# First-layer weights of all eight experts loaded during the routing and kept in SBUF; second-layer weights in two buffers; new order of the splits and additions

## The reference

```python
router_probs = jax.nn.softmax(flat @ router_w + router_b, axis=-1)
topk_probs, topk_idx = jax.lax.top_k(router_probs, 2)
...
# for each of the two experts e of a token, weighted by its probability:
gelu(flat @ rw1[e] + rb1[e]) @ rw2[e] + rb2[e]     # 1024 -> 256 -> 1024
```

## Time and profile before

| | us |
|---|---|
| median of 3 runs | 3153.91 (3153.67 to 3155.99) |
| the profiled execution | 3143.41 |
| its span, first to last instruction | 3141.5 |
| routing in it | 2641 to 2695 |
| expert stage in it | 2696 to 3141.5 |

### The profile page before, as it was taken

How to read it: one execution, slowest core, us unless ns; L and a number is a source line. 1 busy time by engine, 2 the same in 40 slices (tenths; PEclk the granted TensorE clock), 3 DMA queues, 4 the chain that set the end, 5 groups by cost and what they waited for, 6 DMA issues and landing times. The chain is left out here.

```text
span 3141.5 us, 50069 instructions
## 1 busy us (share of the span) xinstructions
PE 2774.9 (88%) x13690; PEld 2153.1 (69%) x13690; DVE 2489.0 (79%) x5349; ACT 1571.3 (50%) x3053; POOL 1639.9 (52%) x1473
## 2 busy tenths in 40 slices
PE   4999969999996997998988999999999595599997
PEld 3788734444445776776766788888888484488886
DVE  8656769999997676577777999999999785577775
ACT  3555623333334525333333677777777451266664
POOL 1788746666663572777773444444444230044443
PEclk9999989999998998999999999999999797699999
DMA  5433489999992032111111778778877551499997
GB/s 184 113 93 107 143 303 347 348 350 353 349 335 59 1 134 55 36 23 23 22 23 34 260 261 259 260 260 261 260 263 255 175 201 58 183 297 297 289 293 194
DMA packets 193609, 609.60 MB, mean 194 GB/s; under 512 B 41979, under 2 KB 51570, under 8 KB 189758
## 3 DMA queue, kind: packets, MB, share of 16 engines
q0 software_dynamic: 135040, 429.23, 43.3%
q1 hardware_dynamic: 58430, 178.63, 16.2%
HBM read 522.69 MB, written 84.86 MB: 193 GB/s over the span
## 5 line engine op out<-in xcount | busy, mean ns | idle before, releaser
L649 POOL DMA_INDIRECT g_rows<-z_rows,edge_src x704 | 696.6, 990 | 608.5 <-PE g_totals L1473 314.7
L1090 POOL DMA_INDIRECT shared<-el_rows,edge_src x352 | 336.7, 957 | 179.6 <-issue 107.0
L690 ACT ACTIVATE g_scaled_hi<-g_rows,edge_weight_sorted 128x1024 fp32r<-128x1024 f32 x176 | 202.7, 1151 | 355.3 <-DMA g_rows<-z_rows,edge_src 345.3
L704 PE MATMUL g_sums<-g_rows,g_share 128*128 128x512 f32 x704 | 332.2, 594 | 22.9 <-DMA g_rows<-z_rows,edge_src 22.9
L1466 PE MATMUL g_sums<-g_rows,g_share 128*128 128x256 f32 x1408 | 348.9, 391 | 0.0
L321 POOL DMA_INDIRECT edge_list<-payload,row_i x196 | 260.6, 1330 | 124.6 <-issue 115.9
L1418 ACT ACTIVATE g_scaled_hi<-g_rows,g_factor 128x256 fp32r<-128x256 f32 x704 | 299.9, 496 | 4.3 <-DMA g_rows<-z_rows,edge_src 2.1
L1542 DVE SCALAR_TENSOR_TENSOR g_scaled_lo<-g_rows,g_factor,g_scaled_hi 128x256 fp32r<-128x256 f32 x704 | 293.4, 479 | 1.7 <-ACT g_scaled_hi L1418 1.6
L1466 PEld LDWEIGHTS g_sums<-g_rows,g_share 128*128 128x128 f32 x1408 | 255.4, 191 | 27.8
L1321 DVE TENSOR_REDUCE t_largest<-t_masked 128x4 f32<-128x512 f32 x352 | 231.5, 685 | 51.9 <-PE t_masked L1172 44.6
L725 DVE SCALAR_TENSOR_TENSOR g_scaled_lo<-g_rows,edge_weight_sorted,g_scaled_hi 128x1024 fp32r<-128x1024 f32 x176 | 225.5, 1281 | 47.3 <-ACT g_scaled_hi L690 44.1
(11 more groups left out here) (396 smaller groups left out, 7494.1 us busy)
## 6 DMA issues: line engine op xcount, KB each, us to landing
e_raw<-in_L_ffn_rw_dram SPq DMA_DIRECT2D x56, 1024.0 KB, 6.8
g_rows<-z_rows,edge_src POOLq DMA_INDIRECT x704, 5.6
z_rows<-z_zout SPq DMA_DIRECT2D x20, 512.0 KB, 3.1
x_rows<-x_all SPq DMA_DIRECT2D x20, 512.0 KB, 2.6
z_rows<-t_zout SPq DMA_DIRECT2D x20, 512.0 KB, 2.7
s_x<-x_rows SPq DMA_DIRECT2D x20, 512.0 KB, 7.1
xn_rows<-s_rows SPq DMA_DIRECT2D x10, 1024.0 KB, 4.1
z_x<-in_x_dram SPq DMA_DIRECT2D x19, 512.0 KB, 4.1
```

Of the source, the lines that this page charges most:

```text
L649: pool.indirect_dma_start(out=r.rows[:, slot, :], out_offset=None, in_=table, in_offset=bass.IndirectOffsetOnAxis(ap=g.src[:, i * GT + q:i ...
L704: nc.tensor.matmul(sums[:, k, h, :], share[:, k, :], r.rows[:, k * GT, h * HALF:(h + 1) * HALF], start=True, stop=False)
L1090: q.indirect_dma_start(out=g.edge_el[:, n, :], out_offset=None, in_=g.el, in_offset=bass.IndirectOffsetOnAxis(ap=g.src[:, n:n + 1], axis=0 ...
```

## The change

- SP loads the first-layer weights of all eight experts (8 loads of 1 MB) in `stage_route`, into `raw1_all`, 64 KB of every partition at the place that `x_all` has left. ScalarE and VectorE wait once, at group 0, for all of them (`g.raw1_in`). The 28 loads of `raw1` are gone.
- ScalarE and VectorE read the first layer of a group's expert out of `raw1_all` at an address from a register, in two halves of 1024 columns. They do so for group s-1, no longer s, and `w1_hi` and `w1_lo` have one buffer: the high part waits for the hidden layer of the group before.
- `raw2` has two buffers; `w2_hi` and `w2_lo` have one and are written in two halves of 1024 columns, again for group s-1, once the outputs of the group before are done.
- The order on ScalarE and VectorE is new, as the rows below show. `rows` moves into the tile `g.shared`, which earlier stages have left. What is computed stays the same.

```diff
+        @block.sync
+        def _(sp):
+            for e in range(EXPERTS):
+                sp.dma_start(g.raw1_all[:, e * KD * EH:(e + 1) * KD * EH].rearrange("p (c f) -> p c f", c=KD),
+                             g.rw1[e].rearrange("(p c) f -> p c f", p=P)).then_inc(g.raw1_in, 16)
...
-        raw1, raw2 = sb("raw1", [P, KD * EH]), sb("raw2", [P, 2 * D])
-        w1_hi, w1_lo = sb("w1_hi", [P, 2, KD, EH], F32R), sb("w1_lo", [P, 2, KD, EH], F32R)
-        w2_hi, w2_lo = sb("w2_hi", [P, 2, 2, D], F32R), sb("w2_lo", [P, 2, 2, D], F32R)
+        raw2 = sb("raw2", [P, 2, 2 * D])
+        w1_hi, w1_lo = sb("w1_hi", [P, KD, EH], F32R), sb("w1_lo", [P, KD, EH], F32R)
+        w2_hi, w2_lo = sb("w2_hi", [P, 2, D], F32R), sb("w2_lo", [P, 2, D], F32R)
...
-                at_least(sp, m.raw1_used, i)
-                sp.dma_start(raw1[:].rearrange("p (c f) -> p c f", c=KD),
...
-                at_least(sp, m.raw2_used, i)
+                at_least(sp, m.w2_low, 2 * (i - 1))
+                sp.dma_start(raw2[:, i % 2, :].rearrange("p (m n) -> p m n", m=2),
...
+            def first_high(i, e, part):
+                at_least(act, m.hidden_ready, 2 * i)
+                s.copy(w1_hi[:, part * PART:(part + 1) * PART, :].rearrange("p c f -> p (c f)"),
+                       g.raw1_all[:, bass.ds(e * KD * EH + part * PART * EH, PART * EH)]).then_inc(m.w1_high, 1)
...
+            def second_high(i, c):
+                act.wait_ge(raw2_in[i % 2], (i // 2 + 1) * 16)
+                at_least(act, m.y_ready, i * GT)
+                s.copy(w2_hi[:, c, :], raw2[:, i % 2, c * D:(c + 1) * D]).then_inc(m.w2_high, 1)
...
+                it, old = item(1), item(2)
+                if it:
+                    e = act.value_load(g.expert[0:1, it.i:it.i + 1], min_val=0, max_val=EXPERTS - 1)
...
+                    token_high(it.i, 0)
+                    first_high(it.i, e, 0)
+                    first_high(it.i, e, 1)
+                    token_high(it.i, 1)
+                    second_high(it.i, 0)
+                if old:
+                    scaled(old.i, 0)
+                if it:
+                    second_high(it.i, 1)
+                if old:
+                    scaled(old.i, 1)
...
+                    low(it.i, 0)
+                    first_low(it.i, e, 0)
+                    first_low(it.i, e, 1)
+                    low(it.i, 1)
...
+                    keep(old.i, 0, shift)
+                    keep(old.i, 1, shift)
+                if it:
+                    second_low(it.i, 0)
+                    second_low(it.i, 1)
                     split_hidden(it.i, 0)
                     split_hidden(it.i, 1)
```

More of the change, by code:

```diff
@@ L2071, in stage_experts @@
         hidden = a.psum("e_hidden", [P, 2, HALF])
-        names = ("bias1_in bias2_in raw1_in raw2_in raw1_used raw2_used w1_high w2_high v_done turned_ready "
+        names = ("bias1_in bias2_in w1_high w1_low w2_high w2_low v_done turned_ready "
                  "hi_ready lo_ready hidden_ready act_ready split_ready y_ready y_kept y_scaled bias1_ready").split()
         m = Named(**{n: a.sem(f"e_{n}") for n in names})
+        raw2_in = [a.sem(f"e_raw2_in{k}") for k in range(2)]
         gathered = [[a.sem(f"e_gathered{k}{q}") for q in range(GT)] for k in range(2)]
         y_added = a.sem("e_y_added")
+        PART = KD // 2
         block = ctx.enter_context(nc.Block())
@@ L2124, in _, with output @@
             t = nc.tensor
-            def output(i, k, q):
+            def output(i, q):
                 def h_part(c):
@@ L2169, in _ @@
             s = nc.scalar
-            def body(item):
[L2172 to L2190, removed]
-                if it:
[L2192 to L2197, removed]
@@ new lines, in first_high, with token_high @@
+            def first_high(i, e, part):
+                at_least(act, m.hidden_ready, 2 * i)
+                s.copy(w1_hi[:, part * PART:(part + 1) * PART, :].rearrange("p c f -> p (c f)"),
+                       g.raw1_all[:, bass.ds(e * KD * EH + part * PART * EH, PART * EH)]).then_inc(m.w1_high, 1)
+            def token_high(i, q):
+                act.wait_ge(m.turned_ready, i * GT + q + 1)
+                at_least(act, m.hidden_ready, 2 * i)
+                s.copy(hi[:, :, q * P:(q + 1) * P],
+                       turned[:].rearrange("p h (c n) -> p (h c) n", n=P)).then_inc(m.hi_ready, 1)
@@ new lines, in scaled @@
+            def scaled(i, q):
+                n = i * GT + q
+                act.wait_ge(m.y_kept, n + 1)
+                s.activation(y_out[:, i % 2, q, :], y_out[:, i % 2, q, :], ACT.Copy,
+                             scale=g.sorted_prob[:, n:n + 1]).then_inc(m.y_scaled, 1)
+            def second_high(i, c):
+                act.wait_ge(raw2_in[i % 2], (i // 2 + 1) * 16)
+                at_least(act, m.y_ready, i * GT)
+                s.copy(w2_hi[:, c, :], raw2[:, i % 2, c * D:(c + 1) * D]).then_inc(m.w2_high, 1)
@@ L2214, in _, with first_low @@
             st = Steps(dve, m.v_done)
+            def first_low(i, e, part):
+                dve.wait_ge(m.w1_high, 2 * i + part + 1)
+                split_vector(v, w1_lo[:, part * PART:(part + 1) * PART, :].rearrange("p c f -> p (c f)"),
+                             g.raw1_all[:, bass.ds(e * KD * EH + part * PART * EH, PART * EH)],
+                             w1_hi[:, part * PART:(part + 1) * PART, :].rearrange("p c f -> p (c f)"), m.w1_low)
             def low(i, q):
@@ L2346, in build @@
             stage_shared_expert(nc, g)
-        stage_route(nc, g)
-        stage_experts(nc, g)
+        g.raw1_in = a.sem("raw1_in")
+        with nc.sbuf_tensor("raw1_all", [P, EXPERTS * KD * EH], F32) as raw1_all:
+            g.raw1_all = raw1_all
+            stage_route(nc, g)
+            stage_experts(nc, g)
 _INS = ['x', 'src', 'dst', 'edge_weight', 'L0_gnn_W', 'L0_ffn_ln1_g', 'L0_ffn_ln1_b', 'L0_ffn_w1', 'L0_ffn_b1', 'L0_ffn_ln2_g', 'L0_ffn_ln2_b', 'L0_ffn_w2', 'L0_ffn_b2', 'L1_gnn_W', 'L1_gnn_a_l', 'L1_gnn_a_r', 'L1_ffn_router_w', 'L1_ffn_router_b', 'L1_ffn_sw1', 'L1_ffn_sb1', 'L1_ffn_sw2', 'L1_ffn_sb2', 'L1_ffn_rw1', 'L1_ffn_rb1', 'L1_ffn_rw2', 'L1_ffn_rb2']
```

58 lines of the change are left out of this document (19 added, 39 removed).

## The result

| | before | after |
|---|---|---|
| median, us | 3153.79 (4 runs, 3149.71 to 3155.99) | 3117.68 (4 runs, 3111.15 to 3118.32) |
| profiled execution | 3143.41 | 3111.15 |

The ratio is 0.9885, with a 95% interval of 0.9867 to 0.9903: 36.1 us less. The forecast was 3112.5, so the kernel is 5.2 us slower than forecast and inside the range. The small miss of the total hides a larger one in one term. I cut both profiled executions at the same events: the start of the routing, the issue of the first gather, the end of hidden layer 0, the end of hidden layer 27, the last instruction.

A forecast was written before the change was run, and what follows sets the result against it. The prediction took DMA, and waits for second-layer weight loads into their only buffer, to bound the kernel. Steps 25.7 plus start 15.7 gave 41.4 us off the median of 3153.91: 3112.5 us, range 3103 to 3124.

The forecast's parts named there:

- The steps: Expert stage, 27 steps: the wait for second-layer weights goes, TensorE alone sets 13.21 us instead of 14.16; gain 25.7 us.
- it would fall if the steps' mean stayed over 13.5: Sign against the forecast in the changed kernel's profile: steps' mean over 13.5 us, or hidden layer 0 ending after 2724.
- The chain that must fit: Token parts and w1 halves between hidden layers: 0.94 to 7.0 fits 7.45 us; rival: too tight, each us costs 27, chance 0.04.
- The start: Up to the end of hidden layer 0: no wait for the second group's weights, end at 2720.4 not 2736.1; gain 15.7 us.
- the upper bound of 3 us: First gather: one load fewer shares the DMA engines, worth at most 3.3 us; taken as 0, with 3 kept for the range.
- The routing: Eight 1 MB loads need 26 to 30 us of 56 with idle DMA engines; cost taken as 0, bounded by 3 us.
- The rival of the paying routing: Routing pays 3 us and more for the loads, and so does the first gather: 3116 to 3120 us, chance 0.08.
- The scatter loop: GpSimd's scatter-adds: loop of 11.9 us fits under 13.21; rival: it binds, steps 13.4 to 14.4, 3118 to 3145 us, chance 0.14.
- The forecast landing of 8.5: Expert stage: scatters land in about 8.5 us, between 10.2 now and 6.2 alone, with half of SP's bytes gone.
- Behind hidden layer 27: Tail from the end of hidden layer 27 to the kernel's end: stays at 23.0 us.
- one case in which plain runs gain more: Rival: waits worth more than profiled in plain runs, or the first gather lands 3 us sooner; 3103 to 3109 us, chance 0.07.

The follow-up runs named there:

- e1: Changed kernel with ScalarE's register load of the next group's expert number moved ahead of the bias copy and activation; step mean 13.20 us, against 13.62.
- e3: Changed kernel with VectorE's first bias addition put back between the two token parts, ahead of the first layer's subtractions; step mean 14.70 us.
- e5: The changed kernel run again, unedited; step mean 13.60 us, median 3555.07 us, ratio to before 0.9889.
- e7: The kernel before with two buffers each for raw1 and raw2 and no other change; step mean 13.57 us, median 3570.0, ratio to before 0.9933.
- e8: Changed kernel with the eight first-layer loads issued at the start of the expert stage, not in the routing; 489.8 us from routing start to end.
- e6: Changed kernel with ScalarE's and VectorE's register loads both moved ahead by a group, run again; step mean 13.19 us, median 3544.56, ratio to before 0.9852.
- e2: Changed kernel with ScalarE's and VectorE's register loads both moved ahead by a group; step mean 13.18 us, median 3549.71, ratio to before 0.9862.
- e4: Changed kernel with scatter-adds cut to 4 columns of 1024 and sent to another tensor; step mean 13.18 us, 455.5 us from routing start to end.
- e10: Changed kernel with one buffer for raw2 in place of two; step mean 13.87 us, 477.1 us from routing start to end.
- e9: Changed kernel with full-width scatters that write rows rather than add; step mean 13.41 us, 464.8 us from routing start to end.

## Why the prediction was nearly right

**The steps: mechanism right, size wrong.** The waits for the second-layer weights went, as forecast. The first step takes 13.19 and all others 13.6 to 13.8. The term was 25.7 us and measured 14.8 (382.4 - 367.6). The step of the prediction that failed is "the register load behind it costs 0.28 and some register operations, which the first transposes, done at 0.90, hide". The earlier trace rows gives the load at its old place in the order, between the second scaling and the bias copy. The change moved it to the head of the next step, where it starts together with the last activation while the two scatters go out. There it takes 1.15. It ends at 1.2 of the step (2799.56 + 0.67 against a start at 2799.06), while the transposes are done at 0.9. Other register operations follow, token half 0 starts at 1.5 for 0.94, the second transposes come after it, and TensorE stands still for 0.4. e1 puts the load back ahead of the bias copy, and steps are 13.20, the forecast's 13.21. The prediction said that it would fall if the steps' mean stayed over 13.5. This part of it did.

**The chain that must fit.** The forecast had 0.45 us of room before the hidden layer. In e1 the last low part starts at 3261.76 and takes 1.22, and the hidden layer starts at 3263.47: 0.49 us. e3 adds 1.2 and a wait of 0.8; less the 0.5 of room that is 1.5 on top of 13.2, and steps are 14.7 (its register load, 0.56, delays nothing). In after the room at token half 1 held; what broke was the room at token half 0, where the prediction only said that the transposes hide the load.

**The start: right.** 15.7 forecast, 16.1 measured (39.5 - 23.4). Hidden layer 0 ended 2.7 us earlier than the 2720.4 of the forecast; 2.2 of these are the earlier stages of that execution. The gather landed in 6.82 where it took 7.8 before, the upper bound of 3 us for it was not needed, and the hidden layer took 7.67 for 7.34.

**The routing: right.** 55.15 for 55.16, with the DMA engines 0.37 busy. The rival of the paying routing is out by the trace.

**The scatter loop: it didn't bind, but its sum was wrong.** The forecast landing of 8.5 against 8.3 is luck. The loop hangs on the landing of the second scatter of a pair. That took 10.1 before and 10.0 after, so it didn't get shorter; only the first's fell, from 10.2 to 6.6. The issue was too low as well: 1.70 in the earlier trace rows is the median of both scatters, and the first by itself took 2.56 before and 1.92 after. From the start of the first to the landing of the second are 12.8 us before and 12.2 after, where the prediction had 11.9 and 10.2. The next pair goes out 1.4 behind that landing in the median and 0.8 at the least, so the loop fits with little to spare. The issues, which the rival had up to 3.2 long, were 1.57 to 1.97. The Trainium skill (DMA: Bandwidth & Descriptors, Queues, rings and completion order), by which queues with work take turns, agrees: the load of `raw2` is issued at 2797.95, behind the first scatter of the pair above and together with the second, and in the last step, where no weights are loaded, the scatters land in 6.2. The same scatters set the forecast off by another way that no rival held: not by their loop, but by what they do to a register load.

**Behind hidden layer 27: nearly.** 24.0 for 23.0. Up to the end of the last scatter's issue both take 10.8. The 1.0 us more lies in its landing (6.7 for 6.2) and the end of the program. The cause is open; the same code ended 23.6 us behind hidden layer 27 in e5.

**From the profile to the median.** The profiled executions differ by 32.3 us, 29.9 of them from the start of the routing on; the medians differ by 36.1. The prediction took the profiled gain off the median and had one case in which plain runs gain more. The terms missed by 11.5 us (470.2 against 458.7). Two differences that no term held took 6.2 of them back. The stages before the routing, which the change doesn't touch, were 2.4 shorter in after's profiled execution. And the profiled execution lay 10.4 under the median of before but only 6.5 under that of after. No run shows a cause for either; the 36.1 us by the medians and the 32.3 by the profiles both lie within the interval of the ratio (31 to 42 us). So the total came out as near as it did by luck. Had the steps been 13.21, the median would have come to 3106.8 (3117.68 - 10.9), 5.7 under the forecast.

## What to carry to other kernels

A duration belongs to its place in the order. When a change moves an instruction, cost it anew at the new place with all that runs beside it there, however small it is: here a load of one number, never over 0.30 us in 28 instances on ScalarE before, cost 10 us. Values that steer a step (register loads of indices) belong a step ahead of their use, where a queue has room. A wait for a load can go by buffers or by fewer bytes: here buffers alone took 16 of 26 us off the steps (e7), and the start gained only because the loads went into a stage with idle DMA engines (e8). A median over two kinds of instances is the time of neither: for a loop, take the instance that closes it (the second scatter's 10.0, not 8.3). The version with both loads early beats both kernels, after by 10.5 us and before by 51.6 in e6 (by 45.3 in e2).

## What the runs showed that I had not expected

**The slow register loads start near a scatter's issue.** I set the start of every such load in the middle of the expert stage against the end of the nearest scatter's issue on GpSimd. "First" and "second" are the scatters of a pair, some 1.9 us apart; durations are medians in us.

| load | its start | us |
|---|---|---|
| before, ScalarE | 3.6 or more ahead of the end of the first | 0.28 |
| e1, ScalarE | 2.6 ahead of the first | 0.28 |
| e3, SP | 0.3 behind the first | 0.27 |
| after, SP | 0.7 behind the first | 1.01 |
| after, ScalarE | 0.5 ahead of the second | 1.15 |
| after, VectorE | 0.4 behind the second | 0.78 |
| e3, ScalarE | 0.5 behind the second | 0.56 |
| e3, VectorE | 1.4 behind the second | 0.32 |
| after, VectorE's other load | 5.6 behind the second | 0.30 |
| e4 (4 columns), SP, ScalarE, VectorE | as in after | 0.27, 0.28, 0.31 |

e10, whose loads drift through the step, has the same pattern: 0.28 at 0.3 behind the first scatter, 0.82 at 0.6, 1.03 at 0.7 and 1.53 at 1.0. So in the middle of the stage the slow stretch begins about 0.4 us behind the end of the first issue, and the loads caught in it are through at the latest 1.1 behind that of the second.

One row doesn't fit: VectorE's load in before mostly stands 0.8 ahead of the end of the second issue, inside the stretch, and takes 0.30 to 1.24 with a median of 0.32. There loads of weights are in flight (DMA engines 0.96 busy). The last steps tell what they do. In before the last weights land at 3097.80; the same load of VectorE, at the same place beside the scatters, then takes 1.24:

```profile
L2240 DVEq TENSOR_LOAD <-group_expert x1: 1243/1243/1243, 3107.3 to 3107.3; - x1
```

In e7 it takes 1.22 and 1.23 in the last two steps. In after the last weights land at 3066.97, and ScalarE's load at 3071.76 still takes 1.17. So the scatters alone suffice, and weights in flight made the load shorter, not longer. That they do so because the scatters' data then come later is argued, not shown. That the scatters' data are needed is shown by e4 (size and target changed together), and that plain writes lengthen register loads too, by e9. By which part of the chip the load is held is open.
